# One wait of the DMA queue, two products of the shared expert and one transposition put elsewhere in a gated cross-attention and expert layer

## What the layer computes

```python
q = heads(layernorm(x) @ Wq.T + bq); k = heads(ctx @ Wk.T + bk); v = heads(ctx @ Wv.T + bv)   # 16 heads of 16
attn = softmax(q @ k.T / 4)                        # per batch and head, 512 x 512
x = x + tanh(g_xattn) * ((attn @ v) @ Wo.T + bo)
h = layernorm(x)
logits = h @ w_router                              # 8 experts, the best 2 of each row
scores = softmax(top_logits)
moe = sum over the 2 chosen e of scores * (silu(h @ fc1[e][:, :256]) * (h @ fc1[e][:, 256:])) @ fc2[e]
shared = (silu(h @ gate_w) * (h @ up_w)) @ down_w  # hidden width 512
x = x + tanh(g_ffn) * (moe + shared)
```

## Time and profile before

| | |
|---|---|
| median of 3 runs | 473.4 us (473.13 to 475.3) |
| the profiled execution | 472.9 us, span 471.2 us |
| around the span | 1.7 us |
| TensorE busy | 461.7 us, 98% of the span |
| VectorE busy | 338.4 us, 72% |
| ScalarE busy | 255.7 us, 54% |
| GpSimd busy | 118.4 us, 25% |
| granted TensorE clock | 1.00 over the span: its upper level, 2.4 GHz |

### The profile page before, as it was taken

The page is one execution under the profiler, slowest core; times in us unless marked ns, Lnnn a source line. Parts: engine busy times, 40 slices in busy tenths (PEclk is TensorE's granted clock), DMA queues, the critical chain, the costliest instruction groups (busy, mean ns, idle before and its releaser), DMA issues.

```text
span 471.2 us, 8172 instructions
## 1 busy us (share of the span) xinstructions
PE 461.7 (98%) x2394; PEld 224.7 (48%) x2394; DVE 338.4 (72%) x858; ACT 255.7 (54%) x544; POOL 118.4 (25%) x143
## 2 busy tenths in 40 slices
PE   8999999999999999999999999999999999999997
PEld 8665422333333333333356564675555555555745
DVE  1888897888888888888847876665565656542574
ACT  1664476777777777777766212113676667631110
POOL 5594485000000000000001177640333223332000
PEclk9999999999999999999999999999999999999999
DMA  8668762956564555320000022232332223211931
GB/s 254 219 179 230 184 198 69 198 141 134 136 134 137 135 134 137 92 69 1 3 1 2 0 102 90 91 110 60 92 87 83 85 87 91 80 57 47 362 114 59
DMA packets 47532, 52.80 MB, mean 112 GB/s; under 512 B 8640, under 2 KB 39744, under 8 KB 47488
## 3 DMA queue, kind: packets, MB, share of 16 engines
q1 hardware_dynamic: 42688, 41.75, 33.1%
q0 software_dynamic: 3168, 8.69, 5.1%
q10 hardware_dynamic: 1632, 1.84, 1.2%
HBM read 34.52 MB, written 17.60 MB: 111 GB/s over the span
## 4 chain that ended last, share of the span: by engine, by line
PE 83%; DVE 6%; DMA 5%; SPq 3%; issue 1%; ACT 1%; POOL 1%; ACTq 0%; POOLq 0%; DVEq 0%
PE PS L1329 12%; PE PS L1241 11%; PE PS L1457 11%; PE PS L1504 10%; PE PS L1611 9%; PE PS L1517 6%; PE PS L1630 5%; PE PS L1606 3%; PE PS L1377 3%; PE PS L1292 3%; PE PS L1625 2%; PE PS L1339 2%; DMA X<-in_x_dram 2%; PE PS L1585 2%; PE PS L1593 2%; DMA q_parts<-R 1%
## 5 line engine op out<-in xcount | busy, mean ns | idle before, releaser
L782 DVE TENSOR_REDUCE nmax<-PS 128x1 f32<-128x512 f32 x256 | 161.8, 681 | 14.7 <-PE PS L1241 14.2
L664 ACT ACTIVATE R<-PS 128x512 f32<-128x512 f32 x256 | 133.2, 603 | 38.9 <-PE PS L1457 38.9
L1241 PE MATMUL PS<-R 96*128 96x512 bf16 x256 | 96.0, 381 | 0.7 <-DMA R<-k_parts 0.5
L1457 PE MATMUL PS<-R 98*128 98x512 bf16 x256 | 86.2, 379 | 1.8 <-DMA R<-mparts 1.5
L1329 PE MATMUL PS<-R 128*32 128x512 f32 x512 | 68.2, 605 | 0.0
L552 POOL DMA_INDIRECT token_y<-R,dest x34 | 32.8, 966 | 86.6 <-DVE R L1124 86.3
L1241 PEld LDWEIGHTS PS<-R 96*128 96x128 bf16 x256 | 24.8, 97 | 56.3 <-DVE nmax L782 39.4
L513 POOL TENSOR_TENSOR rstd<-var_eps,minus_half 128x4 f32<-128x4 f32 x4 | 4.1, 1024 | 187.7 <-DVE var_eps L765 187.7
L1611 PE MATMUL PS<-R 128*128 x100 | 47.3, 595 | 1.0 <-ACT R L738 1.0
L1457 PEld LDWEIGHTS PS<-R 98*128 98x128 bf16 x256 | 24.7, 97 | 41.1 <-ACT R L664 20.9
L683 ACT ACTIVATE R<-PS 128x512 f32<-128x512 f32 x16 | 9.6, 597 | 62.0 <-PE PS L1504 62.0
(11 more groups left out here) (173 smaller groups left out, 602.5 us busy)
## 6 DMA issues: line engine op xcount, KB each, us to landing
R<-q_parts SPq DMA_DIRECT2D x96, 64.0 KB, 3.1
R<-k_parts SPq DMA_DIRECT2D x96, 64.0 KB, 3.2
R<-in_fc_w_dram SPq DMA_DIRECT2D x16, 256.0 KB, 3.0
R<-token_y SPq DMA_DIRECT2D x4, 1024.0 KB, 10.2
R<-slot_x SPq DMA_DIRECT2D x25, 129.0 KB, 2.1
k_parts<-R SPq DMA_DIRECT2D x8, 384.0 KB, 3.2
q_parts<-R SPq DMA_DIRECT2D x8, 384.0 KB, 3.6
fc<-in_fc_w_dram SPq DMA_DIRECT2D x16, 128.0 KB, 3.0
```

The lines of the kernel that those rows point to most:

```text
L664: nc.scalar.activation(PT[:, kt, j, :], PS[:, (G * (TB * i + kt) + j) % 3, :], ACT.Exp).then_inc(exp_done, 1)
L782: nc.vector.tensor_reduce(nmax[:, i % 2, j * TB + qt:j * TB + qt + 1], PS[:, smax_bank(n), :], AX.X, ALU.max, negate=True).then_inc(max_re ...
L1241: mm(PS[:, smax_bank(n), :], QS[g][0:KS, j, qt * P:(qt + 1) * P], KST[g][0:KS, j, :], start=True, stop=True).then_inc(smax_done, 1)
L1457: mm(PS[:, n % 3, :], KST[g][0:KM, j, kt * P:(kt + 1) * P], QS[g][0:KM, j, :], start=True, stop=True).then_inc(st_done, 1)
```

## The change

Three edits, in the order of the program:

1. SP waited for the stored parts of batches 1, 2 and 3 at one place, ahead of `load_max(1)`. Now each batch is waited for ahead of the first `load_group` that reads it (batch 1 ahead of group 4, and so on), and batch 3 also ahead of the first load into the memory that `QP` shares with `fc1`.
2. PE: in batch 3, `router_rows(3)` stands between the gate and the up product of `gate_up(1, 1)` and no longer behind both.
3. PE: of the last chunk of `down(1)`, four products, two stood ahead of `transpose_rows(0)` and two behind it. Now none stands ahead, the first two stand behind it, and the last two stand one each behind `transpose_rows(1)` and `transpose_rows(2)`. DVE's `shared_out(1, 0)` and `shared_out(1, 1)` move into slots 0 and 1, and the five small instructions that scale the routing weights (now `scales`) move from ahead of the slots into slot 2. PE's wait for the freed banks moves from slot 2 to slot 3.

```diff
@@ SP
-            for b in range(1, B):
-                parts_stored(b)
-
             for i in range(GROUPS):
+                if i and (i + 3) % NG == 0 and i + 3 < GROUPS:
+                    parts_stored((i + 3) // NG)
                 if 0 < i and i + 3 < GROUPS:
                     load_group(i + 3)
                 if i + 1 < GROUPS:
...
+                if i == 2:
+                    parts_stored(B - 1)
                 if 2 <= i < 2 + E:
@@ DVE
             tabulate_units()
-            for h in range(2):
-                shared_out(1, h)
-
-            dve.wait_ge(exp_sc, 1)
-            step(nc.vector.tensor_scalar(sc[:, 2, :], sc[:, 1, :], 1.0, None, ALU.add))
...
+            def scales():
+                dve.wait_ge(exp_sc, 1)
+                step(nc.vector.tensor_scalar(sc[:, 2, :], sc[:, 1, :], 1.0, None, ALU.add))
...
                 if j + 1 < SLOTS:
                     destination(j + 1)
+                if j < 2:
+                    shared_out(1, j)
+                if j == 2:
+                    scales()
                 if j >= 2:
-                    slot_result(*divmod(j - 2, UN))
+                    slot_result(j - 2)
@@ PE
             router(3)
-            gate_up(1, 1)
+            gate_or_up(1, 1, 0)
             router_rows(3)
+            gate_or_up(1, 1, 1)
             gate_up(1, 2)
@@ PE
-            down(BE - 1, 2)
+            down(BE - 1, TB)
             transpose_rows(0)
-            down_part(BE - 1, IC - 1, 2)
-            down_part(BE - 1, IC - 1, 3)
+            down_part(BE - 1, IC - 1, 0)
+            down_part(BE - 1, IC - 1, 1)
             for j in range(SLOTS):
                 first_product(j)
...
                     transpose_rows(j + 1)
+                if j < 2:
+                    down_part(BE - 1, IC - 1, 2 + j)
                 if j:
                     transpose_hidden(j - 1)
-                if j == UN - 1:
+                if j == UN:
                     pe.wait_ge(base_ready, 2 * BE)
```

More of the change, by code:

```diff
@@ L1109, in _, with slot_result @@
             tabulate_units()
-            for h in range(2):
-                shared_out(1, h)
-            dve.wait_ge(exp_sc, 1)
-            step(nc.vector.tensor_scalar(sc[:, 2, :], sc[:, 1, :], 1.0, None, ALU.add))
[L1115 to L1123, removed]
+            def scales():
+                dve.wait_ge(exp_sc, 1)
+                step(nc.vector.tensor_scalar(sc[:, 2, :], sc[:, 1, :], 1.0, None, ALU.add))
+                step(nc.vector.reciprocal(sc[:, 3, :], sc[:, 2, :]))
+                step(nc.vector.tensor_tensor(sc[:, 0, :], sc[:, 1, :], sc[:, 3, :], ALU.mult))
+                step(nc.vector.tensor_scalar(scg[:, 0, :], sc[:, 3, :], tg[:, 1:2], None, ALU.mult))
+                step(nc.vector.tensor_scalar(scg[:, 1, :], sc[:, 0, :], tg[:, 1:2], None, ALU.mult))
+            def slot_result(j):
+                u = j % UN
+                dve.wait_ge(y_done, j + 1)
+                wait(dve, y_out[u], j // UN * 16)
                 nc.vector.tensor_copy(YE[:, u, :], PS[:, 5 + u, 0:D]).then_inc(y_ready, 1)
@@ L1173, in _ @@
             for j in (SLOTS - 2, SLOTS - 1):
-                slot_result(*divmod(j, UN))
+                slot_result(j)
             def combine(t):
```

## The result

| | before | after |
|---|---|---|
| median of 9 runs | 473.82 us (473.13 to 475.53) | 472.33 us (471.16 to 473.44) |
| ratio | | 0.9965, 95% interval 0.9948 to 0.9982 |
| the profiled execution | 472.9 us | 472.9 us |
| its span | 471.2 us | 471.2 us |

The kernel gained 0.35%, or 1.65 us of its median, with an interval of 0.85 to 2.5 us (the two medians themselves differ by 1.49 us): right in sign and size. Yet the two profiled executions are equally long. So the profile must be read by places, not by its end. First PE's waits, the view of the earlier trace rows: line, releaser, total, times, longest.

What follows compares the result with a forecast made beforehand. PE was taken to bound the kernel, busy 461.7 of 471.2 us. The three edits' 1.2 + 0.26 + 0 = 1.46, say 1.5 us, gave 473.4 − 1.5 = 471.9 us, range 470.9 to 473.2.

Steps and rivals of the forecast that it cites:

- Edit 1, its place and mechanism: Start of group 1, 71 us: maxima loads no longer wait for stores; PE's stall of 1.25 us goes, 1.2 taken.
- The rival of the loads held up by the stores: Group 1's second load starts its 1.68 us only at the stores' landing: gain there 0.71, total 472.4 us; chance 0.13.
- The rule of the Trainium skill: Semaphore increments land after all earlier writes of that DMA engine: group 1's loads not counted before about 70.0 us.
- both cost nothing: SP's moved waits, ahead of load_group(4) and group 2's first fc1 load: data needed a group's time later, cost 0.
- Edit 2: Start of down(0), 302 us: its wait for hidden(1, 1) goes; count, clearings and first slot's load come 0.26 us earlier.
- Edit 3: Start of the slots, 318 to 325 us: 0.86 us saved becomes PE's wait for the first slot's load; yields about 0.
- The rival that it yields its 0.86: At transpose_rows(0), the transposition didn't wait for the load's landing, so 0.86 us is gained; total 471.0 us; chance 0.12.
- The clearings bind, not the scatters: First slot's load waits for the eight clearings, not POOL's last scatter, so moves by 0.26 us; by 0 otherwise.
- Slower through `scales`: Rival: scales in slot 2 holds up DVE's product of slot 3; at 7.5 us the kernel takes 474.7; chance 0.04.
- The sum: Whole kernel: 1.2 + 0.26 + 0 = 1.46, say 1.5 us gained; chance 0.65 for a gain of 1.2 to 1.8.

Runs made afterwards that it cites:

- e3_edit3: The kernel before with only PE's products of down(1) put behind the transpositions and DVE's moves that go with it; ratio 1.0000 (0.9977 to 1.0022).
- before_again: The kernel before, unchanged, profiled once more; first scores at 37.37 us (36.92 in the first profile), stall ahead of group 1 1.44 us.
- e9: The changed kernel with four waits for stored parts instead of sixteen in SP's loop (41 wait instructions, not 45); ratio to before 0.9954 (0.9938 to 0.9971).
- e10: The changed kernel with six more wait instructions on SP ahead of the table's (51 of them); no timed ratio given, count to load 12.85 us.
- e7: The changed kernel with rank(3) ahead of gate_up(1, 2)'s up product, count ahead of down(0), tabulate ahead of hidden(1, 2); 470.91 us, ratio to before 0.9931.
- e8: The kernel of e7 with PE's products of down(1) put back as before the change, DVE's part kept; 471.67 us, ratio 0.9950 (0.9930 to 0.9969).
- rank_early: The changed kernel with rank(3) on PE amid the pair gate_up(1, 2), ahead of its up product; no timed ratio given, count to load 13.17 us.
- scatter_more: The changed kernel with one more POOL scatter behind the last, awaited by SP ahead of the first slot's load; no timed ratio, count to load 13.47 us.
- e1_edit1: The kernel before with only the waits for the stored parts moved; ratio 0.9983 (0.9962 to 1.0005).

## Why the prediction was right, step by step

- **Edit 1, its place and mechanism: right.** 1.25 us between starts at 72 us (1.2 forecast). The stall is not a fixed quantity, though: measured from the first scores, it was 1.43 (e3_edit3) and 1.61 us (before_again) in the other two profiles without edit 1. The rival of the loads held up by the stores did not come true. By it the second load would have landed 1.68 us behind the last store; it landed 0.33 behind it, and in all ten profiles with edit 1 between 0.33 and 0.90. The rule of the Trainium skill that the prediction quotes (DMA: Bandwidth & Descriptors, Queues, rings and completion order) agrees with these traces: in all ten the first load landed 0.10 to 0.30 us behind the last store and never before it, also where it took 2.2 us for that instead of 1.6. It cost nothing, as both loads were there 0.4 us ahead of PE.
- **Edit 1, the step that failed.** I wrote of the moved waits that "both cost nothing", since what they hold back isn't needed for a group's time. I put at nothing the two instructions themselves. They cost 0.5 us 240 us later: a pause of SP moved ahead of the last clearing, and that clearing landed later (e9 and e10 against the changed kernel; 12.6, 12.85 and 13.1 us from `count` to load).
- **Edit 2: the step right, its effect not.** `hidden(1, 1)` moved out of the way and `down(0)` lost its wait. From the start of the gate product of `gate_up(1, 1)` to `count` it takes 303.55 − 294.29 = 9.26 us, and 303.94 − 294.36 = 9.58 before: 0.32 gained (0.26 forecast). It is the same in every profile where this can be read: 9.25 or 9.26 with edit 2, 9.58 or 9.59 without. The logits were copied at 296.42 and `hidden(1, 1)` started at 299.59, as forecast. In the changed kernel none of it reached the slots: the lengthening on SP took 0.48, more than the 0.32 and another 0.08 between load and first product. In e9, without that lengthening, the slots start 0.41 earlier, so the rest of the forecast path is right. Edit 2 was not run alone.
- **Edit 3: right.** That the first slot's load stood at the very edge, and that the 0.86 us would turn into a wait, is what e3 shows in its profile (a wait of 0.60, 0.09 gained; ratio 1.0000, in an interval too wide to decide). The rival that it yields its 0.86 falls there, and comes true in e7 against e8, where the load is early.
- **The clearings bind, not the scatters: right**, shown by rank_early and scatter_more. In the kernel before it was SP's own run of instructions behind them, and not their landing, that was last.
- **Slower through `scales`: no.** In the profile after, DVE had finished them and the result copy before its product of slot 3 was due:

```profile
328.55 0.17 DVE L1114 TENSOR_SCALAR sc<-sc 128x16 f32<-128x16 f32 x1
...
329.79 0.42 DVE L1124 COPY R<-PS 128x256 f32<-128x256 f32 x1
330.90 0.42 DVE L1162 TENSOR_TENSOR R<-R,PS 128x256 f32<-128x256 f32 x1 [0.69 <-PE PS L1598]
```

- **The sum.** 1.46 us were forecast. The runs say 1.65 (0.85 to 2.5), the profiles, from the first scores on, 282.99 − 281.65 = 1.34. By places: 1.25 at 72 us; 0.17 in the stretch up to `gate_up(1, 1)`, where no edit works and which is chance; then 0.32 + 0.08 − 0.48 = −0.08. So in the changed kernel edit 1 took back at the slots what edit 2 gained, edit 3 gave nothing, and the whole gain is that of 72 us. That the total was right is in part luck: the 0.26 forecast for edit 2 was lost on SP, while the stall that edit 1 removed was on the average of three profiles 1.43 and not 1.2.

## What to carry to other kernels

Ahead of moving work off a critical stretch, look at what the next wait there hangs on: a wait that ends exactly when its engine arrives is not listed as a wait, and issue plus landing time finds it. Here 0.86 us of saved work were worth 0.1 until the load was made early, and 0.86 afterwards. Compare two profiles by the distances between fixed places close to the edit, and not by their spans; one stall of a microsecond in common code hid the whole gain here.

## What the hardware showed that I had not expected

- SP pauses at a fixed count of its own instructions: 0.34 us (0.43 at the first) ahead of every 128th that is recorded, the 80th, 208th, 336th, 464th and 592nd in all 13 profiles, where otherwise at most 0.07 us pass. Two instructions more moved one of these pauses from behind the last of eight clearings to ahead of it, and with what followed it (the clearing landed after 1.9 to 2.1 us and not 1.5) that made `count` to load 0.5 us longer in the changed kernel and 0.8 in e1_edit1.
- A fetch of 8 KB of instructions started 0.6 to 0.8 us behind the end of the pause at the 336th, in all 13. Where it fell 0.5 to 0.7 us behind the start of a small DMA, the last of that DMA's 16 increments came 0.3 to 0.5 us behind the others.
- The first loads of stage 2 vary by 1.5 us from execution to execution of the same code (first scores at 36.78 to 38.27 us).
- Loads of 4 KB issued while the last two stores of 384 KB were under way landed just behind the last store (0.10 to 0.30 us for the first of the two), after 1.6 to 2.2 us; the second took 1.7 to 1.8. In the kernel before, alone, it takes 1.6 and 1.7.
